# A two-layer attention and mixture-of-experts kernel: a scan condition moved into each layer's opening, and score maxima carried as bf16 parts

## The reference, cut to what matters

```
x = x + L0_attention(L0_cond(x, side, side))        # 16 heads of 16, causal softmax
x = x + L0_linear8(L0_cond2(x, side, side))         # both operands rounded to e4m3, then one product
x = x + L1_attention(L1_cond(x, side, side))
x = x + L1_moe(L1_cond2(x, side, side))             # 32 experts, top 6, capacity 384, and a shared expert

def cond(r, k, v):                                  # once for each batch: a "condition"
    ek = exp(min(k, 30));  euk = exp(min(u + k, 30))
    nf, df = forward scan of (ek*v, ek) with the batch's decay
    nb, db = the same scan backward
    return sigmoid(r) * (nf + nb - ek*v + euk*v) / max(df + db - ek + euk, 1e-8) * (0.8 + 0.2*tf)
```

## Time and profile before

| | |
|---|---|
| median of 3 runs | 677.0 us (675.83 to 677.92) |
| the profiled execution, its own time | 678.75 us |
| its span, first to last instruction | 676.9 us |
| busy: PE, DVE, ACT, POOL | 523.4, 432.0, 275.4, 211.8 us |
| opening, to the first maxima | 0 to 42.19 us |
| attention of layer 0, first to last maxima | 42.19 to 168.54 us |
| end of layer 0 and gap, to the first maxima of layer 1 | 168.54 to 219.54 us |
| attention of layer 1, first to last maxima | 219.54 to 341.48 us |
| the rest | 341.48 to 676.9 us |

### The profile page before, as it was taken

How to read it: one execution, slowest core, us unless ns; L and a number is a source line. 1 busy time by engine, 2 the same in 40 slices (tenths; PEclk the granted TensorE clock), 3 DMA queues, 4 the chain that set the end, 5 groups by cost and what they waited for, 6 DMA issues and landing times.

```text
span 676.9 us, 12242 instructions
## 1 busy us (share of the span) xinstructions
PE 523.4 (77%) x4564; PEld 407.6 (60%) x4564; DVE 432.0 (64%) x834; ACT 275.4 (41%) x557; POOL 211.8 (31%) x169
## 2 busy tenths in 40 slices
PE   0278799998716779999875689169999999999950
PEld 0156566665404456666654355059999999999940
DVE  3748699999882779999936833036566566566510
ACT  3323464654533445454534111024444444444420
POOL 2000000000012000000000577705778777687772
PEclk9999799999966999999996599679999999999995
DMA  7999910000000000000003233275997869769423
GB/s 279 267 219 223 227 47 1 2 2 1 1 1 0 1 2 1 2 1 2 2 1 135 91 116 110 98 225 143 220 216 197 221 163 228 210 174 225 108 23 68
DMA packets 56716, 71.97 MB, mean 106 GB/s; under 512 B 11777, under 2 KB 45036, under 8 KB 56544
## 3 DMA queue, kind: packets, MB, share of 16 engines
q1 hardware_dynamic: 40272, 57.48, 30.2%
q0 software_dynamic: 16400, 13.87, 11.1%
HBM read 42.22 MB, written 37.04 MB: 117 GB/s over the span
## 4 chain that ended last, share of the span: by engine, by line
PE 49%; DVE 26%; issue 9%; POOL 7%; ACT 5%; DMA 2%; POOLq 0%; SPq 0%; DVEq 0%
PE S L894 14%; DVE negmax L1095 8%; PE PJ L907 8%; POOL xe_rows L358 6%; PE OB L907 4%; PE TB L879 3%; PE S L692 3%; PE S L706 2%; DVE both L979 2%; PE PJ L676 2%; PE S L702 2%; PE PJ L638 2%; DVE fwd L967 2%; PE S L688 2%; PE S L710 2%
## 5 line engine op out<-in xcount | busy, mean ns | idle before, releaser
L894 PE MATMUL S<-xgT,wgu_s 128*128 128x384 f32 x576 | 108.6, 341 | 1.2 <-DVE hidden_f L1336 1.2
L358 POOL DMA_INDIRECT xe_rows<-x_tok,slot_i x48 | 47.2, 984 | 182.5 <-ACT x_tok L577 168.1
L894 PEld LDWEIGHTS S<-xgT,wgu_s 128*128 128x128 f32 x576 | 99.3, 189 | 1.5 <-issue 1.4
L369 POOL DMA_INDIRECT out<-sig,y_token x48 | 75.9, 1581 | 46.6 <-ACT sig L612 33.9
L1095 DVE TENSOR_REDUCE negmax<-S 128x4 f32<-128x512 f32 x64 | 58.3, 952 | 46.0 <-PE S L692 34.1
L369 POOL DMA_INDIRECT odd_out<-sig,y_token x48 | 76.6, 1595 | 24.4 <-ACT sig L612 12.3
L445 ACT ACTIVATE prob<-S 128x1536 f32<-128x1536 f32 x32 | 46.4, 1449 | 66.1 <-PE S L710 66.1
L907 PE MATMUL PJ<-x8m,hidden_f 128*128 128x256 f32 x256 | 60.5, 379 | 1.4 <-ACT sig L612 1.4
L1333 DVE TENSOR_TENSOR hidden_f<-ek,S 128x384 f32<-128x384 f32 x32 | 17.7, 554 | 56.9 <-ACT ek L595 56.9
L907 PEld LDWEIGHTS PJ<-x8m,hidden_f 128*128 128x128 f32 x256 | 47.9, 190 | 6.7 <-issue 1.8
L346 POOL PARTITION_ALL_REDUCE amax_x<-amax_x x1 | 0.4, 380 | 162.2 <-DVE amax_x L1085 162.2
(11 more groups left out here) (178 smaller groups left out, 1018.0 us busy)
## 6 DMA issues: line engine op xcount, KB each, us to landing
xe_rows<-x8m SPq DMA_DIRECT2D x4, 3468.0 KB, 41.9
ratio<-xe_rows SPq DMA_DIRECT2D x32, 433.5 KB, 4.1
ek<-in_wgu SPq DMA_DIRECT2D x32, 384.0 KB, 4.6
x8m<-in_wd SPq DMA_DIRECT2D x32, 256.0 KB, 2.9
x<-in_x SPq DMA_DIRECT2D x1, 1024.0 KB, 7.3
odd_out<-x8m SPq DMA_DIRECT2D x1, 1024.0 KB, 29.3
out<-side SPq DMA_DIRECT2D x8, 128.0 KB, 5.5
out<-odd_out POOLq DMA_DIRECT2D x1, 1024.0 KB, 7.9
```

The source lines that it names most:

```text
L358: eng.indirect_dma_start(xe_rows, bass.IndirectOffsetOnAxis(slot_i[:, t, k:k + 1], 0), x_tok[:, t, :], None, bounds_check=ROWS - 1, oob_is ...
L369: eng.indirect_dma_start((out, odd_out)[j % 2], bass.IndirectOffsetOnAxis(y_token[:, j, t:t + 1], 0), ye_sb[:, j % 2, t, :], None, bounds_ ...
L894: ins = eng.matmul(S[:, m, 0:CAP], fast(wgu_s[:, j % 2, a, k, m * P:(m + 1) * P]), fast(xgT[:, j % 2, b, k, :]), start=n == 0, stop=n == N ...
```

## The change

Five things are done together. In the diff, the first two added lines stand at the end of ACT's opening, the first `condition_input` at the end of DVE's opening, and the loop with `k_mm(1, 0)` is that of the 8-bit products.

1. **Ratios move.** `condition_input` is a whole ratio with gate and product, outside the loop. One (layer 0, batch 1) is put at the end of the opening, one (layer 1, batch 2) at the end of the gap. Layer 0's attention still has eight ratios (its inputs for batches 2 and 3, four of `L0_cond2`, two of layer 1), layer 1's has five instead of seven, all in its first ten steps.
2. **Projections.** In every batch the next batch's q stands in step `u = 0` and its k in `u = 1`; `cst` has three buffers. At the start of a layer k comes before q, k is written to `OB` and q to `PJ`, and the first scores wait for the first part of `q_sb` alone. In layer 1 both stand on PE before the last of the four 8-bit products.
3. **Gap.** The residual of the 8-bit layer moves from POOL to DVE.
4. **Maxima.** `negmax` has 8 numbers a partition for a step. Four operations on POOL (`split_maxima`) split them into three bf16 parts; `neg_mm` is three bf16 matmuls instead of two float32 ones, `neg_rows` is bf16, and one bf16 matmul a head of 384 columns adds all three parts.
5. **Masks.** The mask is put only on the two diagonal blocks: 8 matmuls of 128 columns behind the scores, instead of 4 of 384 ahead of them.

```diff
+            spread_decay(0, 1, 1, 1)
+            bonus_exp(0, 1, 1, 1)
...
             def ratio_of(L, b, u):
             r = 2 * b + u // 2
-            if L and r == 2 * B - 1:
-                return None
-            i, bb = (0, r + 1) if r < B - 1 else (1, r - B + 1) if r < 2 * B - 1 else (2, 0)
-            n = 1 + r + 2 * B * L
-            return i + 2 * L, bb, n, n % 2
+            n = (2, 2 * B + 3)[L] + r
+            i, bb = (((0, 2), (0, 3), (1, 0), (1, 1), (1, 2), (1, 3), (2, 0), (2, 1)),
+                     ((2, 3), (3, 0), (3, 1), (3, 2), (3, 3), None, None, None))[L][r] or (None, None)
+            return None if i is None else (i, bb, n, n % 2)
...
         @block.gpsimd
-            for b in range(B):
-                eng.wait_ge(sem("y8_made"), b + 1)
-                eng.tensor_tensor(x[:, :, tok(b)], x[:, :, tok(b)], y8[:, :, tok(b)], ALU.add).then_inc(sem("x_res_8"), 1)
+            def split_maxima(L, v):
+                at = 4 * (B * QUADS * L + v)
+                eng.wait_ge(sem(f"max_{L}"), v + 1)
+                if v >= 2:
+                    eng.wait_ge(sem(f"neg_mm_{L}"), v - 1)
+                settle(eng, "pool")
+                eng.tensor_copy(neg_parts[:, v % 2, :, :, 0], negmax[:, v % 2, :, :]).then_inc(sem("split"), 1)
+                eng.wait_ge(sem("split"), at + 1)
+                eng.tensor_tensor(neg_rest[:, :, :], negmax[:, v % 2, :, :], neg_parts[:, v % 2, :, :, 0], ALU.subtract)\
+                   .then_inc(sem("split"), 1)
+                eng.wait_ge(sem("split"), at + 2)
+                eng.tensor_copy(neg_parts[:, v % 2, :, :, 1], neg_rest[:, :, :]).then_inc(sem("split"), 1)
+                eng.wait_ge(sem("split"), at + 3)
+                eng.tensor_tensor(neg_parts[:, v % 2, :, :, 2], neg_rest[:, :, :], neg_parts[:, v % 2, :, :, 1], ALU.subtract)\
+                   .then_inc(sem("split"), 1)
...
         @block.tensor
+            def mask_diagonals(turned):
+                for i in range(HPT):
+                    for lo in (0, 2 * P):
+                        ins = eng.matmul(S[:, i, lo:lo + P], ident_b[:, :], causal_b[:, turned, :], start=False,
+                                         stop=lo > 0, skip_group_check=True)
+                return ins
...
             def neg_mm(L, v):
-                eng.wait_ge(sem(f"max_{L}"), v + 1)
+                eng.wait_ge(sem("split"), 4 * (B * QUADS * L + v + 1))
...
             for b in range(B):
+                if b == B - 1:
+                    k_mm(1, 0)
+                    q_mm(1, 0)
                 eng.wait_ge(sem("x8q_done"), b + 1)
...
         @block.vector
+            condition_input(0, 0, 1, 1, 2, "sig_made", 1)
...
+            def residual_8(b):
+                eng.wait_ge(sem("y8_made"), b + 1)
+                eng.tensor_tensor(x[:, :, tok(b)], x[:, :, tok(b)], y8[:, :, tok(b)], ALU.add).then_inc(sem("x_res_8"), 1)
             for b in range(B):
                 eng.wait_ge(sem("x8_scaled"), b + 1)
                 quantise(x8[:, :, tok(b)], c_all[:, :, tok(b)], x8m[:, :, tok(b)], "x8q", 3 * b)
-            eng.wait_ge(sem("v_mm_0"), B)
-            apply(cst[:, 0, :, :], 2, 0, "c_ready_1", "sig_8", 1, 2 * B + 1)
+                if b:
+                    residual_8(b - 1)
+                if b >= 2:
+                    apply(cst[:, b - 2, :, :], 2, b - 2, "c_ready_1", "sig_8", b - 1, 2 * B + b - 1)
+            residual_8(B - 1)
+            condition_input(1, 2, 2, 2 * B + 2, B + 1, "sig_8", 3)
             attention(1)
```

More of the change, by code:

```diff
@@ L246, in ratio_at @@
         def ratio_at(i, b):
-            return ratio[:, i // 2, :, tok(b)] if i % 2 else ratio[:, 1, :, tok(B - 1)]
+            return ratio[:, i // 2, :, tok(b if i % 2 else B - 1 - b)]
         def by_batch(t):
@@ L343, in _ @@
                .then_inc(sem("gmax_w"), 1)
+            eng.wait_ge(sem("neg_parts_zeroed"), 1)
+            for v in range(B * QUADS):
+                split_maxima(0, v)
             eng.wait_ge(sem("amax_x"), B)
@@ L347, in _ @@
                .then_inc(sem("gmax_x"), 1)
-            for b in range(B):
-                eng.wait_ge(sem("y8_made"), b + 1)
-                eng.tensor_tensor(x[:, :, tok(b)], x[:, :, tok(b)], y8[:, :, tok(b)], ALU.add).then_inc(sem("x_res_8"), 1)
+            for v in range(B * QUADS):
+                split_maxima(1, v)
             eng.wait_ge(sem("slots_zeroed"), 80)
@@ L565, in _ @@
             eng.preload_act_table_set("natural_log_exp_and_others")
+            spread_decay(2, 2, 2 * B + 2, 0)
+            bonus_exp(2, 2, 2 * B + 2, 0)
             attention(1)
@@ L684, in scores @@
                     eng.wait_ge(sem(f"k_out_{L}"), b + 1)
+                if v == 0:
+                    eng.wait_ge(sem(f"q_part_{L}"), 1)
+                if v == 1:
+                    eng.wait_ge(sem(f"q_out_{L}"), 1)
                 if v >= 2:
                     eng.wait_ge(sem(f"exp_{L}"), v - 1)
-                for i in range(HPT):
-                    eng.matmul(S[:, i, 0:3 * P], ident_b[:, :], causal_b[:, 0, :], start=True, stop=False)
                 for st, cols in HALVES:
@@ L691, in scores @@
                         rows = slice(i * SLOT, (i + 1) * SLOT)
-                        ins = eng.matmul(S[:, i, cols], q_sb[rows, b % 2, u, st * P:(st + 1) * P],
-                                         k_sb[rows, b % 2, u // 2, 0:P * (st + 1)], start=False, stop=st == 1)
-                ins.then_inc(sem(f"score_{L}"), 1)
+                        eng.matmul(S[:, i, cols], q_sb[rows, b % 2, u, st * P:(st + 1) * P],
+                                   k_sb[rows, b % 2, u // 2, 0:P * (st + 1)], start=st == 0, stop=False,
+                                   skip_group_check=True)
+                mask_diagonals(0).then_inc(sem(f"score_{L}"), 1)
             def turned_scores(L, v):
@@ L701, in turned_scores @@
                 for i in range(HPT):
-                    eng.matmul(S[:, i, 0:3 * P], ident_b[:, :], causal_b[:, 1, :], start=True, stop=False)
+                    rows = slice(i * SLOT, (i + 1) * SLOT)
+                    eng.matmul(S[:, i, 0:3 * P], pick[rows, :], neg_rows[rows, v % 2, :], start=True, stop=False,
+                               skip_group_check=True)
                 for kt, (q_cols, cols) in enumerate(((slice(0, T), slice(0, T)), (slice(P, T), slice(T, 3 * P)))):
@@ L760, in attention @@
                             pv(L, v - 1)
-                        if b == 0 and u == 2:
-                            q_mm(L, 1)
                         turned_scores(L, v)
@@ L1078, in _, with condition_input @@
             eng.wait_ge(sem("ek_made"), 2)
+            def condition_input(L, i, b, n, ngate, sigmoid, nsig):
+                buf = n % 2
+                bonus_arg(i, b, n, buf)
+                scan_forward(i, b, n, buf, 0)
+                scan_backward(n, buf, 0)
+                denominator(i, b, n, buf)
+                scan_forward(i, b, n, buf, 1)
+                scan_backward(n, buf, 1)
+                numerator(b, n, buf)
+                refine(n)
+                gate(b, n, sigmoid, nsig)
+                next_input(L, b, n, ngate)
+            condition_input(0, 0, 1, 1, 2, "sig_made", 1)
             def condition(L, b):
@@ L1174, in attention @@
                                 refine(n)
-                                if i == 2 * L and bb:
+                                if i == 2 * L:
                                     gate(bb, n, *(("sig_made", 1), ("sig_8", bb + 1))[L])
-                                    next_input(L, bb, n, bb + 1 if L == 0 else B + bb)
+                                    next_input(L, bb, n, bb + 1 if L == 0 else B + bb - 1)
                                 else:
@@ L1387, in layout @@
     causal = np.where(np.arange(P)[None, :] > np.arange(P)[:, None], -1e30, 0.0)
-    a["causal"] = np.stack([np.concatenate([m, np.zeros((P, P)), m], 1) for m in (causal, causal.T)], 1).astype(bf16)
+    a["causal"] = np.stack([causal, causal.T], 1).astype(bf16)
     proj = f32["L1_attn_w_project"]
```

100 lines of the change are left out of this document (51 added, 49 removed).

## The result

The changed kernel takes 703.19 us (median of 5 runs, 701.07 to 712.99), the kernel before 677.92 beside it: ratio 1.0356 [1.0315, 1.0397], 25 us slower. One of the five runs, that of 712.99 us, is left out of the ratio, as it is over 1.5% above the fastest. The forecast was 688 with 673 to 697, so the time lies above the range. The sign and the mechanism that gave it were right, one stage was not. The profiled execution's own time is 705.54 us, its span 703.7 us.

A forecast was written before the change was run, and what follows sets the result against it. Ahead of the experts' stage, DVE was taken to bound steps without a projection, PE those with one. Terms 9.2 - 6.7 + 6.2 + 9.9 - 6.9 - 0.8 = +10.9 gave 688 us against the median of 677.0, range 673 to 697.

The forecast's parts named there:

- Opening, 0: Before layer 0's first maxima: the moved ratio (10.9 us) fits into DVE's 11.59 us of idle time, change 0.
- The first splits: First to second maxima take 13.2 us in each layer, 7.4 of it POOL's code load: +9.2 and +9.9 us.
- The rival that the load costs little: Bare ISA behind the first copy costs 1.7 us or runs ahead: 5.7 us less per layer, 676.5; chance 0.16.
- POOL beside DVE: Split operations take turns with DVE's: split ends 3.55 us after the maxima in odd steps, 2.3 in even, 1.0 alone.
- short operations of the bonus: In even steps these DVE operations come first after the maxima, so the split ends after 2.3 us.
- The loops, layer 0: Second to last maxima of layer 0: steps at the longer of DVE's and PE's sums, 114.8 against 121.5, -6.7 us.
- Layer 1, -6.9: Second to last maxima of layer 1: 110.9 against 117.8 us, the last four steps at 7.3 and 6.8.
- Gap, +6.2: Between the layers' attention: DVE's roundings, residuals and remaining ratio put layer 1's first maxima at 225.2 to 226 against 219.54.
- PE's early k and q save nothing here: In the gap, k and q ahead of the fourth 8-bit product bring no saving, as DVE is last.
- Masks: On PE per step: turned scores 2.34 to 1.9, transposition 0.64 to 0.25, scores 1.56 to 1.5; bounds 0.4 to 1.0 us.
- The signs: What would show it: POOL idle some 7 us before its first small product, second maxima 13 us behind, split spread over 2 to 4.
- The rival of both costs absent: Neither POOL's turns beside DVE nor the code load costs as forecast: 665 us, faster by 1.8%; chance 0.04.

The follow-up runs named there:

- e7: The kernel before with one edit of the change, masks only on the two diagonal blocks behind the scores: 668.37 us, ratio 0.9855.
- e2: The changed kernel plus one small two-input POOL operation behind each all-reduce, ahead of the first split: 685.85 us, ratio 1.0112.
- e9: The changed kernel plus 24 unread bf16 products ahead of TensorE's split wait, both layers, all steps but the first: 700.05 us, ratio 1.033.
- e1: The changed kernel with float32 maxima again, without the bf16 parts and POOL's split: 670.55 us, ratio 0.988 to the kernel before.
- e6: e1 with layer 1's k and q behind the fourth 8-bit product and the decay spread ahead of the table load: 665.20 us, ratio 0.981.
- e10: e2 plus 24 unread bf16 products ahead of the split wait, layer 0 from the third step, layer 1 third to eleventh: 679.02 us, ratio 1.001.
- e4: e2 plus 24 unread bf16 products ahead of the split wait in layer 0, all steps but the first: 685.38 us, ratio 1.0071.
- e3: The changed kernel with the four split operations on DVE behind the maxima, none on POOL: 684.15 us, ratio 1.008 to the kernel before.

## Why the prediction was right and where it failed

Measured changes by stage: -1.3, +8.7, +7.7, +6.3, +9.0, -4.4, +0.8, together +26.8 us of span.

- **Opening, 0: right in kind.** The ratio fitted; the first maxima came 1.3 us earlier, now straight behind DVE's last product, so the ratio sets them. That PE's work was cover held only because PE was slow: in `e7`, without the ratio, the first maxima came at 38.37. Where the scores are short, the moved ratio costs 3.0 us there.
- **The first splits: right.** 13.58 and 13.13 us for 13.2, the bare ISA at 7.42 and 6.96 us for 7.4. `e2` showed the cause, not just the place: with the code loaded ahead, 6.8 us of each stall went. The rival that the load costs little fell.
- **POOL beside DVE: right in the lock and wrong by 0.9 us in even steps.** The split ends 3.3 us behind the maxima in odd steps (forecast 3.55; 2.2 in the two with a residual) and 3.2 in even ones (2.3). The "short operations of the bonus" are one of 0.6 us, in whose time POOL gets only its first operation through; the scan that follows holds the second (1.19 us), the next scan the fourth (1.12). Where no ratio runs the four take 1.1 us (forecast 1.0). The Trainium skill's lock ("SBUF — State Buffer", Who interferes with whom) is what these rows show.
- **The loops, layer 0, "Sum 114.8 against 121.5: -6.7": this is the step that failed.** It came out at 129.11, +7.7. Its steps were costed with TensorE at full clock, "PE with a projection: 1.83 + split + 0.25 + 1.73 + 1.5 + gaps", while its own times for the split put a pause of 1.65 us (3.55 less 1.9 for the turned scores) into PE's queue in every odd step; what a pause does to the clock it put at nothing, without a reason. At full clock the loop is 118.57 us (`e9`), so that 10.5 us of the 14.3 are the clock and 3.8 the rest, above all the even steps' split. That is the traced execution, with a mean clock of 0.879; three of the other runs had 0.886 and took 701.07 to 703.19 us, so the clock's part is likely smaller in them. The forecast had counted a low clock only behind the two code loads.
- **Layer 1, -6.9: too good by 2.5 us**, by the same even steps above all, as the clock fell there in no more than one projection; the four last steps came at 6.5 to 6.9 us, 0.3 to 0.5 under the forecast's 6.8 and 7.3. (Its signs speak of six such steps; its sum has four.)
- **Gap, +6.2: right**, 57.33 us for 57.4 (the gap's 51.0 and 6.2, and 0.2 for the end of layer 0; its terms add up to first maxima at 224.9 to 225.5, and not to the 225.2 to 226 that it gives), with the two waits that the sum had named (2.86 us for the fourth `y8`, 2.39 us for the decay). "PE's early k and q save nothing here" was too kind: their place ahead of the fourth product costs 2.4 of the 2.99 us that `e1` shows.
- **Masks.** Their worth was put at the bounds 0.4 to 1.0 us a step together with the rest; alone they are 0.48, and 10.2 us in the kernel's median, ratio 0.9855, of which the opening's clock is a part.
- **The signs.** The forecast's signs were there: some 7 us ahead of POOL's first small product in each layer, second maxima 13 us behind the first, transpositions that wait. The rival of both costs absent ("665") has its counterpart in `e1`, 670.6: what the moves and masks are worth without the split. That `e6` gives 665.2 is chance, as it has two mends of the gap besides. In the chances, the terms named give 0.72 for slower and 0.20 for faster, where 0.71 and 0.19 stand.

That TensorE's pauses bring the clock down is what `e9` and `e10` show: they only fill those waits with work, and behind a filled wait no projection is slow. Left open is why it falls behind one pause and not behind another: with equal waits (1.71 and 1.72 us) layer 1's steps kept the clock in the changed kernel and lost it in `e2`, and in `e4` the mean clock of the same program came out at two levels. The Trainium skill ("TensorE: Matmul & The Clock Gate", A second HAM failure mode: psum-queue depth-cycling) tells of a kernel in which frequent short pauses between groups of matmuls make the clock swing between its two levels. These traces agree, with pauses of 1.6 to 1.7 us (2.2 to 2.8 in `e3`).

## What to carry to other kernels

Before a small step is put on another engine inside a ring, add up its wait on the engine that it feeds: four operations of 0.2 us became 3.2 us beside the other engine's scans, and the pause that they made in TensorE's queue cost its clock as well. Price a bundle of edits one by one: here one edit (short masks) was worth 10 us, part of it the clock's, one (parts) cost some 30, and the moved work gained nothing until TensorE's part was short and two waits in the gap were mended. If a swap of POOL's code must be, put it where POOL waits for nobody who is waited for.

## What the runs showed of the hardware that was not expected

- TensorE's clock falls to half (1.2 GHz of 2.4) inside a loop without any long stall. A projection then takes 3.3 to 3.5 us for 1.95, and the next scores are at full clock again (0.94 us). Before it fell the engine had run a group of masks (0.62 us) and then waited 1.6 to 1.7 us, or in `e3` waited 2.2 to 2.8 us ahead of the turned scores. Equal waits in the same traces left the clock up.
- Whether it falls differs between executions of one program: 678.3 to 679.1 and 685.4 to 686.8 us in `e4`; in `e10`, with the waits filled, ten runs within 4.4 us.
- Ahead of the first two-input operation behind an all-reduce POOL is idle for 6.90 to 8.15 us, wherever the operation stands (7.46 in the kernel before, 7.42 and 6.96 in the changed one), also when a copy with a cast has run between them. That copy itself starts with its input.
- A POOL operation of 8 numbers takes 0.20 to 0.23 us alone, 0.95 to 1.19 us when a scan of DVE runs, and ends with it. On DVE the same operations take 0.17 to 0.20 us.
